# Masking query tile 1 of an attention max pass on VectorE: one fused instruction a head in place of a shared plain maximum

## The chip, the cores and the metric

The kernel runs on one core of a Trainium2 chip. The metric is the device time of one execution in microseconds, as the median of several executions. The core's engines are TensorE (PE in the profile; PEld is its weight load), VectorE (DVE), ScalarE (ACT), GpSimd (POOL) and SyncE (SP), which issues the DMAs. Each runs its own list of instructions in order, and they wait for one another at semaphores.

## The reference

Eight sequences of 512 tokens with 256 features go through one transformer block with its norms behind the sums:

```
qkv = x @ Wqkv + bqkv                      # 16 heads of 16
scores = q @ k.T / 4 + alibi_causal_bias   # -(i-j)*slope for j <= i, -inf for j > i
attn = softmax(scores) @ v
x1 = layernorm(x + attn @ Wo + bo)
up, gate = x1 @ ternary(W_up).T, x1 @ ternary(W_gate).T
out = layernorm(x1 + (silu(up) * gate) @ ternary(W_down).T)
```

The causal mask is what matters here: query i must not see key j > i, neither in the sum nor in the maximum that the softmax subtracts.

## The kernel before

Each batch (one sequence) goes through two passes of scores. The **max pass** computes each query's largest score, the exp pass computes the scores again, transposed, with that maximum already subtracted by rows of the stacked operands, and takes the exponential.

The heads go in four quads of four. In the max pass of a quad the scores of a head and of one tile of 128 queries are one product: queries on the 128 partitions, the keys 0 to 128 * (tile + 1) - 1 along the columns, so 128, 256, 384 or 512 columns. Function `max_unit` groups these into 11 units a quad, each filling a PSUM bank as far as it goes: unit 0 is query tile 0 of all four heads (4 x 128 columns), units 1 and 2 are query tile 1 of two heads each (2 x 256), units 3 to 6 are tile 2 of one head (384), units 7 to 10 tile 3 of one head (512). Step `max.G.N` is the products of unit N in quad G on TensorE (L477), step `take.G.N` the maximum on VectorE. Two banks, `max_bank0` and `max_bank1`, take the units in turn: TensorE waits for `max_drained` of the unit two before, VectorE for `max_filled` of its own.

Only the last 128 columns of a unit's head cross the diagonal. They are masked in one of two ways, by the constant `MASK_BY_DVE`:

- For query tiles below it TensorE adds the mask: behind each head's product it multiplies an identity by a 128x128 tile `causal` (0 or -1e30) into the last 128 columns (L480). VectorE then takes one plain maximum over the whole unit, a `tensor_reduce` with as many results as heads (L731).
- For query tiles from it on, VectorE adds `causal_wide` (bf16, the mask in its last 128 columns and 0 before) and takes the negated maximum in one fused instruction, `tensor_tensor_reduce` (L727). The sums are written back into the bank, and the maximum is fetched by a second, short instruction, the accumulator read, which the profile lists at the same line and which gives the bank back.

When all 11 units of a quad are taken, `mt.G` transposes the maxima on TensorE (L489), `mt_out.G` splits them in two bf16 parts on VectorE (L741, L743), and SyncE copies them into `q_stack` for the exp pass of that quad.

The order of work on all engines is one list written out by hand: `FIRST_ORDER` for the first batch, `LOOP_ORDER` for batches 1 to 7, each of which also ends the batch before (its last exponentials, the products with v, output projection, norms, feed-forward part), `LAST_ORDER` for that tail alone. Each engine walks the list and does its own part of each step. Around quads 0 to 2 the list interleaves the max pass with the feed-forward steps of the batch before: `up.M` and `gate.M` on TensorE (L555), `swish.M` (L784) and `swiglu.M` (L794) on VectorE, `down.M` on TensorE (L568) into the two accumulator banks; `qk_rest` and `x1_hi` parts on ScalarE, `x1_lo` (L776) and `v_out` (L714) on VectorE. Around quads 2 and 3 it interleaves the exp pass of quads 0 and 1 (L495 on TensorE, L610 on ScalarE, masks by GpSimd at L855) and `pv`, the products with v (L508). All banks but the two max banks and the two accumulators are a ring of four, used in list order; each is given back by the instruction that empties it. In the loop, for instance, `gate.4` takes the bank that `gate.3` had and `swiglu.3` emptied.

A few lines of the loop's order around the change, quad 1 to quad 3:

```
down.0 max.1.2 swish.2 take.1.0 gate.3 swiglu.2 ... mt.0 take.1.1 take.1.2 ... swish.3 ... max.1.3 up.4
max.1.4 take.1.3 up.5 max.1.5 stack_read.1 swiglu.3 gate.4 max.1.6
up.7 take.1.10 exp.0.2 take.2.0 exp.0.3 swiglu.5 take.2.1 max.2.3 take.2.2 load_next max.2.4 gate.6
mt_out.2 take.3.1 max.3.2 exp.1.2 take.3.2 exp.1.3 max.3.3 exp.1.4 down.7
```

Of the kernel before, what the change touches and what calls it, by code (L numbers as in the profile page):

```python
# [11 lines left out]
ALU = mybir.AluOpType  # L12
# [4 lines left out]
BATCH, SEQ, HID = 8, 512, 256  # L17
# [11 lines left out]
LOWEST_START = 3e38  # L29
# [11 lines left out]
GROUP = 40  # L41

RING = 4
MASK_BY_DVE = 2
EXP_UNITS = 10
MAX_UNITS = 11

# [1 line left out]
def max_unit(n):  # L49

    if n == 0:
        return [0, 1, 2, 3], 0
    if n < 3:
        return [2 * (n - 1), 2 * (n - 1) + 1], 1
    return ([n - 3], 2) if n < 7 else ([n - 7], 3)
# [95 lines left out]
def block_kernel(nc, x, w_qkv, b_qkv, b_qkv_cols, w_o, b_o, w_up_t, w_gate_t, w_down_t, k_const, q_const, out, scratch):  # L151
    ctx = ExitStack()
    with ctx:
        def sb(name, shape, dt):
            return ctx.enter_context(nc.sbuf_tensor(name, shape, dt))

        def sem(name):
            return ctx.enter_context(nc.semaphore(name))
# [13 lines left out]
        causal_wide = sb("causal_wide", [P, SEQ], BF16)  # L172
# [15 lines left out]
        neg_max = sb("neg_max", [P, QUADS, P], F32)  # L188
# [28 lines left out]
        max_bank = [ctx.enter_context(nc.psum_tensor(f"max_bank{i}", [P, 512], F32)) for i in range(2)]  # L217
# [6 lines left out]
        max_drained = [sem(f"max_drained{i}") for i in range(2)]  # L224
# [99 lines left out]
        def max_at(g, n):  # L324

            u = g * MAX_UNITS + n
            return u % 2, u // 2
# [101 lines left out]
        def _(pe):  # L429
            def body(steps, it):  # L430
# [3 lines left out]
                for step in steps:  # L434
# [30 lines left out]
                    elif kind == "max":  # L465
# [9 lines left out]
                        for i, h in enumerate(heads):  # L475
                            o = max_bank[k][:, width * i:width * (i + 1)]
                            mm = pe.matmul(o, q_stack[0:MAX_ROW, 4 * g + h, P * tile:P * (tile + 1)],  # L477
                                           k_stack[0:MAX_ROW, 4 * g + h, 0:width], start=True, stop=tile >= MASK_BY_DVE)
                            if tile < MASK_BY_DVE:
                                mm = pe.matmul(o[:, width - P:width], ident_bf[:, :], causal[:, :], start=False, stop=True)  # L480
# [165 lines left out]
        def _(dve):  # L646
# [29 lines left out]
            def body(steps, it):  # L676
# [3 lines left out]
                for step in steps:  # L680
# [23 lines left out]
                    elif kind == "pv" and step[1] >= 2 and step[2] == TT - 1:  # L704
                        g = step[1]
# [11 lines left out]
                    elif kind == "take":  # L717
                        _, g, n = step
                        k, use = max_at(g, n)
                        heads, tile = max_unit(n)  # L720
                        width = P * (tile + 1)
                        at_least(dve, max_filled[k], MAX_PER_BANK, it, use + 1)
                        first_col = 4 * heads[0] + tile
                        if tile >= MASK_BY_DVE:
                            dve.sem_inc(dve_passed, 1)
                            scores = max_bank[k][:, 0:width]
                            dve.tensor_tensor_reduce(  # L727
                                scores, scores, causal_wide[:, SEQ - width:SEQ], -1.0, LOWEST_START, ALU.add, ALU.min,
                                neg_max[:, g, first_col:first_col + 1]).then_inc(max_drained[k], 1)
                            continue  # L730
                        dve.tensor_reduce(  # L731
                            neg_max[:, g, first_col:first_col + 4 * (len(heads) - 1) + 1:4],
# [2 lines left out]
                    elif kind == "mt_out":  # L735
                        g = step[1]
# [8 lines left out]
                    elif kind == "nt_out":  # L745
                        g = step[1]
# [3 lines left out]
                        heads = rg.bank(nt)[:, :].rearrange("p (s c) -> p s c", c=32)  # L750
# [74 lines left out]
                    elif kind == "ternary" and step[1] < 2:  # L825
                        i = step[1]
# [5 lines left out]
                                                 op0=ALU.is_gt, op1=ALU.subtract).then_inc(ternary_done, 1)  # L832

            iterations(dve, body)


# [137 lines left out]
```

## Time and profile before

| | |
|---|---|
| runs of the kernel | 634.56 us median of 3 (634.03 to 636.05) |
| the profiled execution | 636.64 us, span in the profile 634.7 us |
| mean granted TensorE clock | 0.967 of full |
| PE busy | 582.3 us, 92% of the span |
| DVE busy | 502.0 us, 79% |
| ACT busy | 307.1 us, 48% |
| POOL busy | 296.5 us, 47% |

Busy times are averages over stages with different limits. A record of an instruction reaches from its start to the acknowledged end of its writing, and the next one often starts before that; start-to-start times tell how long an engine is really held. Times of the timeline are in microseconds from the span's start.

### The profile page before, as it was taken

Reading aid. Unit: us, or ns where it says so; the run is one execution under the profiler, and the core shown is the slowest. Engines: PE = TensorE matmul, PEld = TensorE weight load, DVE = VectorE, ACT = ScalarE, POOL = GpSimd, SP = SyncE. Lnnn points to the kernel's source line nnn. Section 1 sums busy time; section 2 is a strip of 40 time slices with the busy share of each in tenths; the row PEclk is TensorE's granted clock in tenths of the full one; section 3 lists DMA queues with packets and bytes.
Section 4 is the critical chain, followed back from the end, with each engine's and each line's share of the span. In section 5 each row is a group of like instructions: output and inputs, shape, how many; then the busy total and the mean of one; then the engine's idle time right before and its main releaser. Section 6 shows DMA issues by size and latency. Waiting matters only on the chain.

```text
span 634.7 us, 13198 instructions
## 1 busy us (share of the span) xinstructions
PE 582.3 (92%) x4027; PEld 339.6 (54%) x4066; DVE 502.0 (79%) x1271; ACT 307.1 (48%) x543; POOL 296.5 (47%) x494
## 2 busy tenths in 40 slices
PE   6477899999999999999999999999999999998694
PEld 3243346664656556664656556664656656663343
DVE  4367968997699968997699968997699968995454
ACT  1144542477245742387245743477245743477151
POOL 1307683274544563264544563264544563275233
PEclk9767999999999999999999999999999999999987
DMA  8952155502761065502761065502761065502000
GB/s 212 311 191 65 35 166 169 134 3 75 215 174 34 1 193 171 133 1 69 221 174 34 1 198 166 133 1 74 216 174 34 1 207 158 133 1 68 1 1 33
DMA packets 48096, 69.42 MB, mean 109 GB/s; under 512 B 4784, under 2 KB 44208, under 8 KB 44976
## 3 DMA queue, kind: packets, MB, share of 16 engines
q1 hardware_dynamic: 48080, 69.22, 37.3%
q8 instruction: 8, 0.13, 0.1%
q14 instruction: 8, 0.07, 0.0%
HBM read 39.59 MB, written 29.36 MB: 109 GB/s over the span
## 4 chain that ended last, share of the span: by engine, by line
PE 59%; DMA 15%; DVE 13%; issue 6%; ACT 3%; POOL 2%; SPq 1%; POOLq 0%; DVEq 0%
PE ring L555 18%; PE max_bank L477 10%; DMA k_stack<-k_slots 9%; PE acc L568 8%; PE ring L495 6%; PE ring L457 5%; PE acc L508 5%; DMA k_slots<-qk_parts 3%; PE max_bank L480 2%; DMA q_stack<-max_parts 2%; DVE y L660 2%; PE ring L462 1%; DVE qk_rest L690 1%; DVE qk_rest L699 1%; POOL rstd L881 1%
## 5 line engine op out<-in xcount | busy, mean ns | idle before, releaser
L610 ACT ACTIVATE probs<-ring 128x512 f32<-128x512 f32 x320 | 171.4, 601 | 88.2 <-PE ring L495 55.4
L855 POOL TENSOR_SCALAR_AFFINE_SELECT probs<-probs 128x256 f32<-128x256 f32 (+1 forms) x320 | 121.1, 403 | 165.2 <-ACT probs L610 164.1
L727 DVE CUSTOM_DVE_ANT_0 max_bank<-max_bank,causal_wide 128x384 f32<-128x384 f32 (+1 forms) x256 | 158.3, 636 | 9.5 <-PE max_bank L477 6.8
L477 PE MATMUL max_bank<-k_stack,q_stack 112*128 112x384 bf16 (+3 forms) x512 | 137.3, 312 | 20.8 <-DMA k_stack<-k_slots 11.8
L885 POOL TENSOR_TENSOR hidden_lo<-hidden,hidden_hi 128x512 f16<-128x512 f32 x64 | 74.1, 1159 | 77.1 <-ACT hidden_hi L640 76.9
L495 PE MATMUL ring<-q_stack,k_stack 128*128 128x128 bf16 (+3 forms) x473 | 93.9, 297 | 6.8 <-DMA q_stack<-max_parts 5.3
L477 PEld LDWEIGHTS max_bank<-k_stack,q_stack 112*128 112x128 bf16 x512 | 50.6, 99 | 61.9 <-DVE neg_max L727 21.5
L629 ACT ACTIVATE gating<-ring,tanh_scale 128x512 f32<-128x512 f32 x64 | 44.0, 687 | 74.6 <-PE ring L555 74.6
L508 PE MATMUL acc<-probs,v_ones 128*32 128x512 f32 (+3 forms) x1024 | 78.2, 437 | 0.1
L495 PEld LDWEIGHTS ring<-q_stack,k_stack 128*128 128x128 bf16 x512 | 46.5, 100 | 57.2 <-issue 21.2
L731 DVE TENSOR_REDUCE neg_max<-max_bank 128x2 f32<-128x512 f32 (+1 forms) x96 | 63.3, 686 | 13.4 <-PE max_bank L480 13.1
L457 PE MATMUL ring<-x_t,wqkv 128*128 128x512 f32 x128 | 63.1, 619 | 1.6 <-DVE x_t L684 1.2
L568 PE MATMUL acc<-tern_down,hidden_hi 128*128 128x256 f16 x256 | 59.0, 272 | 0.4
L568 PE MATMUL acc<-tern_down,hidden_lo 128*128 128x256 f16 x256 | 59.0, 272 | 0.0
L508 PEld LDWEIGHTS acc<-probs,v_ones 128*32 128x32 f32 x1024 | 28.4, 109 | 42.0 <-issue 36.4
L784 DVE SCALAR_TENSOR_TENSOR gating<-gating,ring 128x512 f32<-128x512 f32 x64 | 43.1, 683 | 4.7 <-ACT gating L629 4.5
L794 DVE SCALAR_TENSOR_TENSOR hidden<-gating,ring 128x512 f32<-128x512 f32 x64 | 43.7, 682 | 3.6 <-POOL hidden_lo L885 2.6
L640 ACT ACTIVATE hidden_hi<-hidden 128x512 f16<-128x512 f32 x64 | 40.2, 628 | 9.8 <-DVE hidden L794 9.7
L480 PE MATMUL max_bank<-causal,ident_bf 128*128 128x128 bf16 x256 | 44.4, 227 | 0.0
L601 ACT ACTIVATE qk_parts<-ring,bias_cols 128x512 bf16<-128x512 f32 x16 | 11.0, 688 | 66.7 <-PE ring L457 66.7
L881 POOL TENSOR_TENSOR rstd<-var_eps,half_neg 128x4 f32<-128x4 f32 x16 | 16.3, 1019 | 53.0 <-DVE var_eps L674 53.0
L555 PE MATMUL ring<-x_hi,tern_up 128*128 128x512 f16 x128 | 39.0, 386 | 0.7 <-issue 0.7
(93 smaller groups left out, 877.6 us busy)
## 6 DMA issues: line engine op xcount, KB each, us to landing
q_stack<-qk_scratch SPq DMA_DIRECT2D x16, 768.0 KB, 5.9
k_stack<-k_slots SPq DMA_DIRECT2D x16, 768.0 KB, 8.2
qk_scratch<-qk_parts SPq DMA_DIRECT2D x16, 384.0 KB, 5.2
k_slots<-qk_parts SPq DMA_DIRECT2D x16, 384.0 KB, 3.2
xin<-x_dram SPq DMA_DIRECT2D x9, 512.0 KB, 3.5
qk_scratch<-qk_parts SPq DMA_DIRECT2D x16, 256.0 KB, 2.8
k_slots<-qk_parts SPq DMA_DIRECT2D x16, 256.0 KB, 3.0
res<-x_dram SPq DMA_DIRECT2D x8, 512.0 KB, 4.0
```

The costliest lines, as they stand in the source:

```text
L457: mm = pe.matmul(bank[:, :], wqkv[:, f, col:col + P], x_t[:, f, :], start=(f == 0), stop=(f == FT - 1))
L477: mm = pe.matmul(o, q_stack[0:MAX_ROW, 4 * g + h, P * tile:P * (tile + 1)], k_stack[0:MAX_ROW, 4 * g + h, 0:width], start=True, stop=tile ...
L480: mm = pe.matmul(o[:, width - P:width], ident_bf[:, :], causal[:, :], start=False, stop=True)
L495: mm = pe.matmul(bank[:, col:col + SEQ - P * j], k_stack[:, 4 * g + h, P * j:P * (j + 1)], q_stack[:, 4 * g + h, P * j:SEQ], start=True, s ...
L508: mm = pe.matmul(acc[g % 2][32 * h:32 * (h + 1), P * j:SEQ], v_ones[:, j, 4 * g + h, :], probs[:, g % 2, n, col:col + SEQ - P * j], start= ...
L555: mm = pe.matmul(bank[:, :], w[:, f, P * m:P * (m + 1)], part[:, f, :], start=(f == 0 and part is x1_hi), stop=(f == FT - 1 and part is x1 ...
L568: mm = pe.matmul(acc[t // 2][:, HID * (t % 2):HID * (t % 2 + 1)], part[:, m, P * t:P * (t + 1)], tern_down[:, m, :], start=(m == 0 and par ...
L610: rg.drained(act.activation(probs[:, g % 2, n, :], rg.bank(step)[:, :], ACT.Exp), step)
L727: dve.tensor_tensor_reduce(scores, scores, causal_wide[:, SEQ - width:SEQ], -1.0, LOWEST_START, ALU.add, ALU.min, neg_max[:, g, first_col: ...
L731: dve.tensor_reduce(neg_max[:, g, first_col:first_col + 4 * (len(heads) - 1) + 1:4], max_bank[k][:, 0:width * len(heads)].rearrange("p (h ...
L855: return pool.affine_select(out=v, in_=v, compare_op=ALU.is_ge, fill=0.0, base=0, pattern=([[0, blocks]] if blocks > 1 else []) + [[1, P]] ...
L885: pool.tensor_tensor(hidden_lo[:, m, :], hidden[:, m % 2, :], hidden_hi[:, m, :], ALU.subtract).then_inc(hidden_split, 1)
```

## The change

The constant goes from 2 to 1, and VectorE's branch goes over the heads of a unit, since a fused instruction gives one maximum only. For units 1 and 2 of each quad TensorE issues the two products without the two mask products, and VectorE issues two fused instructions of 128x256, one for each head, in place of one plain maximum over 128x512. The bank is given back by the second one. Unit 0 keeps TensorE's mask and the plain maximum; tiles 2 and 3 are as before. The order of steps is not changed.

```diff
-MASK_BY_DVE = 2
+MASK_BY_DVE = 1
...
                         if tile >= MASK_BY_DVE:
                             dve.sem_inc(dve_passed, 1)
-                            scores = max_bank[k][:, 0:width]
-                            dve.tensor_tensor_reduce(
-                                scores, scores, causal_wide[:, SEQ - width:SEQ], -1.0, LOWEST_START, ALU.add, ALU.min,
-                                neg_max[:, g, first_col:first_col + 1]).then_inc(max_drained[k], 1)
+                            for i in range(len(heads)):
+                                scores = max_bank[k][:, width * i:width * (i + 1)]
+                                ins = dve.tensor_tensor_reduce(
+                                    scores, scores, causal_wide[:, SEQ - width:SEQ], -1.0, LOWEST_START, ALU.add, ALU.min,
+                                    neg_max[:, g, first_col + 4 * i:first_col + 4 * i + 1])
+                            ins.then_inc(max_drained[k], 1)
                             continue
```

## Rows read from the trace of the kernel before

**Rows 1.** The page: busy tenths in 40 slices, then the chain by engine.

```profile
PE   6477899999999999999999999999999999998694
DVE  4367968997699968997699968997699968995454
...
PE 59%; DMA 15%; DVE 13%; issue 6%; ACT 3%; POOL 2%; SPq 1%; POOLq 0%; DVEq 0%
```

**Rows 2.** Busy time in windows: first batch's front, one loop batch, its middle.

```profile
core 0: us, PE busy (x) PEld busy (x) DVE busy (x) ACT busy (x) POOL busy (x), PEclk, DMA share, GB/s
27.00:95.00 68.00, 55.68 (x345) 27.27 (x350) 50.40 (x120) 30.52 (x52) 37.10 (x49) 0.83 0.42 134
315.00:387.00 72.00, 70.54 (x510) 42.02 (x514) 61.58 (x160) 37.41 (x67) 34.72 (x60) 1.00 0.38 111
322.00:342.00 20.00, 19.95 (x132) 11.86 (x133) 19.86 (x52) 8.55 (x14) 5.66 (x6) 1.00 0.51 142
```

**Rows 3.** Timeline of PE, quad 2: start, length, line, operation, tiles, shapes.

```profile
341.58 0.22 PE L480 MATMUL max_bank<-causal,ident_bf 128*128 128x128 bf16 x1
341.64 0.59 PE L555 MATMUL ring<-x_hi,tern_up 128*128 128x512 f16 x2
...
342.93 0.49 PE L477 MATMUL max_bank<-k_stack,q_stack 112*128 112x384 bf16 x2
...
344.14 0.34 PE L477 MATMUL max_bank<-k_stack,q_stack 112*128 112x384 bf16 x1
```

**Rows 4.** Timeline of PE, quad 0 of the first batch.

```profile
28.04 0.31 PE L480 MATMUL max_bank<-causal,ident_bf 128*128 128x128 bf16 x1
28.15 0.42 PE L477 MATMUL max_bank<-k_stack,q_stack 112*128 112x256 bf16 x1
```

**Rows 5.** Groups of instructions, shapes apart: busy us, mean ns, idle before.

```profile
L727 DVE CUSTOM_DVE_ANT_0 max_bank<-max_bank,causal_wide 128x512 f32<-128x512 f32 x128 | 87.8, 705 | 1.9 <-PE max_bank L477 0.3
...
L727 DVE CUSTOM_DVE_ANT_0 max_bank<-max_bank,causal_wide 128x384 f32<-128x384 f32 x128 | 71.1, 567 | 7.5 <-PE max_bank L477 6.5
...
L731 DVE TENSOR_REDUCE neg_max<-max_bank 128x2 f32<-128x512 f32 x64 | 42.1, 684 | 0.8 <-PE max_bank L480 0.8
```

**Rows 6.** Timeline of DVE, quad 2.

```profile
340.47 0.69 DVE L731 TENSOR_REDUCE neg_max<-max_bank 128x4 f32<-128x512 f32 x1
...
341.66 1.29 DVE L731 TENSOR_REDUCE neg_max<-max_bank 128x2 f32<-128x512 f32 x2
343.45 0.57 DVE L727 CUSTOM_DVE_ANT_0 max_bank<-max_bank,causal_wide 128x384 f32<-128x384 f32 x1 [0.51 <-PE max_bank L477]
343.94 0.14 DVE L727 DVE_READ_ACCUMULATOR2_ANT neg_max<- 128x1 f32 x1
343.94 0.60 DVE L727 CUSTOM_DVE_ANT_0 max_bank<-max_bank,causal_wide 128x384 f32<-128x384 f32 x1
...
344.45 0.68 DVE L784 SCALAR_TENSOR_TENSOR gating<-gating,ring 128x512 f32<-128x512 f32 x1
```

**Rows 7.** Timeline of DVE, quad 1.

```profile
330.52 1.28 DVE L731 TENSOR_REDUCE neg_max<-max_bank 128x2 f32<-128x512 f32 x2
331.72 0.68 DVE L784 SCALAR_TENSOR_TENSOR gating<-gating,ring 128x512 f32<-128x512 f32 x1
...
332.79 0.68 DVE L794 SCALAR_TENSOR_TENSOR hidden<-gating,ring 128x512 f32<-128x512 f32 x1
...
333.86 0.14 DVE L727 DVE_READ_ACCUMULATOR2_ANT neg_max<- 128x1 f32 x1
334.06 0.57 DVE L727 CUSTOM_DVE_ANT_0 max_bank<-max_bank,causal_wide 128x384 f32<-128x384 f32 x1
```

**Rows 8.** Timeline of PE, quad 1.

```profile
333.70 0.60 PE L555 MATMUL ring<-x_hi,tern_gate 128*128 128x512 f16 x2
```

**Rows 9.** Timeline of DVE, quad 3.

```profile
351.65 1.28 DVE L731 TENSOR_REDUCE neg_max<-max_bank 128x2 f32<-128x512 f32 x2
```

**Rows 10.** Timeline of PE, quad 3.

```profile
352.48 0.33 PE L477 MATMUL max_bank<-k_stack,q_stack 112*128 112x384 bf16 x1
```

## The prediction

> **What bounds the kernel now.** I read the page first, for the mix of engines over time. Outside the start and the end TensorE's slices read 9. VectorE reads 9 too, in three or four slices of each batch: those in which the max pass and the feed-forward part overlap. The chain that ended last is TensorE's for 59% and VectorE's for 13% [rows 1]. Then the windows: the first batch ran at a mean granted clock of 0.83, with TensorE waiting often; a loop batch (315 to 387) ran at 1.00 and shows 70.5 us of busy TensorE and 61.6 us of busy VectorE in 72.0; in its overlapping part, 322 to 342, they show 19.95 and 19.86 us of the 20 [rows 2]. Such figures are inflated, because a record overlaps the next one: a 128-column mask product has a record of 0.22 us, and yet the next matmul starts 0.06 us after it [rows 3]. So I went by start-to-start times, in the timeline of that one batch (batch 4 of 0 to 7; the other loop batches repeat it within hundredths). There too each engine starts one instruction straight behind another, with pauses of 0.2 us at most. Two engines are full at once, and they hand two score banks back and forth in a fixed order. So what decides is not which engine has less work, but at which hand-off one waits for the other.
>
> **What goes.** Per batch 16 products of the causal tile for query tile 1 (2 units x 2 heads x 4 quads), each 0.06 us of TensorE at full clock (341.58 to 341.64 [rows 3]); I take 0.058, the mean over a row of them. That is 0.23 us per quad, 0.93 per batch, 6.5 over seven batches. In the first batch a mask takes 0.11 us (28.04 to 28.15 [rows 4]), the lower clock level, so 1.7 us there: 8.2 us in all for 128 mask products.
>
> **What comes.** 64 plain maxima of 128x512 (684 ns each [rows 5]) give way to 128 fused instructions of 128x256, which the trace does not have. The nearest rows are 384 wide (567 ns) and 512 wide (705 ns) [rows 5]: 138 ns for 128 elements, so a record of 429 ns at 256 wide. The next instruction starts 0.08 us before a fused record ends (343.45 + 0.57 = 344.02 against the next start at 343.94 [rows 6]), so the slot is 0.345 us. A fused instruction directly behind a fused one takes some 0.02 to 0.04 us longer (0.49, then 0.51 us from 343.94 to 344.45 [rows 6]); I take 0.035. A unit of two heads then occupies VectorE for 0.345 + 0.035 + 0.345 = 0.725 us, where the plain maximum takes 0.60 (two of them have a common record of 1.29 us, one alone of 0.69 [rows 6]). The two units of a quad follow each other, mostly with nothing between: 0.725 + 0.035 + 0.725 = 1.485 us in place of 1.20, so +0.285 per quad, +1.1 per batch. The lower bound of the new slot is its 256 elements alone, 0.276 us (a gain of 0.05 per unit against 0.60); the upper bound is the slot of the 384-wide one, 0.49 (+0.38 per unit). I take 0.345, since two rows give a line through it.
>
> The bank is given back later too. A plain maximum gives it back with its record, 0.69 us after its start. A fused one gives it back with its accumulator read, which starts where the slot ends and takes 0.14 us [rows 6]; TensorE's next product into that bank starts 0.06 us later (343.45 + 0.49 + 0.14 = 344.08, product at 344.14 [rows 3]). For the pair that is 0.345 + 0.38 + 0.14 = 0.865 us after its start, 0.18 later than now. No DMA, no bank and no wait is added; what changes is how late existing waits clear.
>
> The Trainium skill (Perfetto Trace Analysis, Optimizing Scalar/DVE Operations) puts a VectorE instruction's overhead on PSUM at about 125 ns and advises grouping. Here the rows leave 0.07 us (0.345 less 0.276). With the page's figure each half would take 0.40 us and the forecast below would be about 1.6 us later; this trace does not agree with it, and the sum goes by the rows.
>
> **Through one batch, quad by quad** (shifts against now).
>
> Quad 0: VectorE's extra 0.25 us falls beside ScalarE's x1_hi, for which VectorE waits before x1_lo, and TensorE's x_lo part of up.0 waits for that in turn. Two masks fewer stand ahead of qk.3, which feeds that ScalarE work. I take half of their 0.12 us: -0.06. Without that cover the 0.25 us would arrive in full.
>
> Quad 1: take.1.1 starts at 330.52 and VectorE is never idle from there to 334. Swish.3 (331.72) and swiglu.3 (332.79) come 0.285 us later [rows 7]. Swiglu.3 now ends at 333.47 (332.79 + 0.68) and frees the ring bank that gate.4 takes at 333.70 [rows 8]; it would end at 333.76, plus 0.06 for the hand-off: 333.81. So TensorE comes out of quad 1 about 0.10 us late, its 0.23 us of saved slots used up in waiting. VectorE's pause of 0.2 us (from 333.86, where an accumulator read starts that any next instruction could run beside, to 334.06 [rows 7]) takes in the rest of its delay, and both engines are at +0.10.
>
> Quad 2: take.2.1 starts at 341.66, and take.2.2 gives its bank back at 341.66 + 1.29 = 342.95 [rows 6]. Max.2.4, the second of the pair of products at 342.93, starts at 343.10, straight behind max.2.3 (a common record of 0.49, where one of 384 columns has 0.34 alone) [rows 3]. After the change take.2.2 starts 0.76 us after take.2.1 and gives back 0.865 us later: 343.29, the product at 343.35, +0.25; with the 0.10 from quad 1 it is +0.35. TensorE could have been there 0.23 us early; that is lost, and gate.6 and down.4 stand in the queue right behind it.
>
> Quad 3: take.3.1 starts at 351.65 [rows 9], with the shift at 352.00. Its bank is wanted by max.3.3 at 352.48, which starts as TensorE's queue comes to it [rows 10]. After the change: 352.00 + 0.865 + 0.06 = 352.93, so +0.44. Behind it stand exp.1.4 and down.7; down.7 ends the accumulators, which first the second norm and then pv.0 need, and TensorE has no room before pv.0 at 355.4.
>
> From pv.0 the chain goes over ScalarE, GpSimd's masks and rstd, VectorE's normalised output, mt_out.3 and its DMA to the next batch's first products. I found no pause in TensorE's timeline there that could take the delay in, so I carry it over whole. Per batch: 0.44 - 0.06 = +0.38; over seven, +2.7 us.
>
> First batch: at the lower clock a mask is worth 0.11 us, and the maxima of a quad's two-head units wait for their own products. Removing four masks per quad (0.43 us) pays for the 0.285 us more of VectorE. But the third quad waits for a stack transfer and the last one runs at full clock. I take 0; ends -1.7 (all masks) and +1.1. The last pass has no max work: 0.
>
> Sum: the profiled execution took 636.6 us around a span of 634.7; with +2.7 it would be 639.3 around 637.4. Its own time is 2.1 us above the median of the runs, 634.56, so the forecast for the median is 634.56 + 2.7, which I round to **637.2**.
>
> **Rivals.** About 0.3% (1.9 us) is what this kernel's measurement can tell from no change; below, "same" is within that.
>
> 1. *Hand-offs, as above*: chance 0.43. Own range 635.9 to 639.5: lower if half of each shift is taken in, upper if the quads' shifts add undiminished.
>
> 2. *VectorE paces the whole max pass*: every 0.285 us arrives, 32 quads x 0.285 = 9.1, giving 643.7. For it: VectorE's full windows [rows 2]. Against: its pause of 0.51 us before 343.45, a wait for TensorE [rows 6], and others of 0.2 us behind it. It decides if these close. Chance 0.13.
>
> 3. *Both effects cancel*: TensorE's saved 0.93 us per batch fills the waits that VectorE's later releases make, 634.6 (within 1.5). It holds if VectorE arrives in quad 2 some 0.3 us ahead of where it does now, or if the pair releases its bank after 0.7 us. Chance 0.25.
>
> 4. *TensorE paces, faster*: the slots saved in quads 0 and 1 reach the end, 8 x 0.058 x 7 = 3.2 us, plus 0.9 in the first batch: 630.5; with all four quads, 8.2 us, 626.4. For it: TensorE's 9s in almost every slice and its 59% of the chain [rows 1]. Against: max.2.4 and max.3.3 start within 0.16 us of their banks' release today (342.95 to 343.10, 352.34 to 352.48) [rows 3, 6, 9, 10]. It decides where VectorE has room at those places. Chance 0.19. The Trainium skill (TensorE: Matmul & The Clock Gate, Back-to-back issue gap) gives about 81 ns per 128-column matmul in a stream with weight loads. That would make this rival's full gain 9 us in the loop instead of 6.5; the rows here say 0.06 us, so the trace does not agree.
>
> That the masks would stay on TensorE can't be: both sides of the edit go by the same constant.
>
> **How the numbers follow.** Predicted is rival 1's 637.2. Slower by over 0.3%: nearly all of 1 and all of 2, 0.54. Same: 3 and a little of 1, 0.27. Faster: 0.19. The range of 631.0 to 641.5 leaves out most of 2 and the larger gains of 4, under 0.2 together.
>
> **What would show it.** 128 fused records of 128x256 near 430 ns, some 0.38 us apart within a pair; mask products down to 128. In each loop batch max.2.4 and max.3.3 start 0.06 us behind an accumulator read, with a TensorE gap of 0.3 us or more before them, and gate.4 behind swiglu.3. VectorE's pauses near 343 and 353 shrink. The period from batch to batch, 71.4 us (max.0.0 starts at 172.75 in batch 2 and at 458.28 in batch 6), would become about 71.8. The prediction is wrong if the 256-wide slot is far from 0.345 us, if TensorE shows no new gap at those three places, or if a gap elsewhere, in the part behind pv.0, takes the delay in.

## The result, and the profile after

The changed kernel takes 659.37 us in the median (656.6 to 665.02), the kernel before 634.48: 1.0387 times, with a 95% interval of 1.0348 to 1.0426. That is 25 us more between the medians, nine times what was forecast, and far outside the range. The profiled execution took 659.4 us around a span of 657.3, where before it was 636.64 around 634.7.

The page of the changed kernel, lines that answer to [rows 1], and the lines on the queues that carry instructions:

```profile
PE   6367899998999899998999989998999989999694
...
DVE  4386859996699758996699958995699957996454
...
q14 instruction: 38, 0.31, 0.2%
q8 instruction: 8, 0.13, 0.1%
...
PE 59%; DVE 20%; issue 12%; DMA 6%; DVEq 1%; POOL 1%; ACT 1%; SPq 1%; POOLq 0%
```

and the same queues on the page of before:

```profile
q8 instruction: 8, 0.13, 0.1%
q14 instruction: 8, 0.07, 0.0%
```

Both pages look alike where I had looked. What differs is a line that I had not read: q14 brought 38 packets of instructions (8 KB each: 0.31 MB over 38) in place of 8, and the chain spends 12% of the span in "issue", where it was 6% [rows 1]. Of these two only the queue's line holds up as a sign: the experiments below have kernels with 9 packets and 11% "issue", and others with 38 or 39 packets and 7 or 8%. The DMA view of the window from 160 to 590 us, which lies inside the loop, from its second turn on, says when the packets come. For the kernel before it has no line for q14 at all; for the changed kernel it has this one, and three of the packets start within 226 to 233, around a jump back that is looked at below:

```profile
q14 instruction: 26, 0.21, 0.2%
```

The groups by shape, with the new form (compare [rows 5]):

```profile
L728 DVE CUSTOM_DVE_ANT_0 max_bank<-max_bank,causal_wide 128x256 f32<-128x256 f32 x128 | 50.9, 453 | 0.2
```

A 256-wide record takes 453 ns, where the line through two rows said 429; two in three directly follow a fused one and are the longer kind. Quad 2 of the batch that [rows 6] showed, VectorE:

```profile
353.43 0.42 DVE L728 CUSTOM_DVE_ANT_0 max_bank<-max_bank,causal_wide 128x256 f32<-128x256 f32 x1
353.77 0.14 DVE L728 DVE_READ_ACCUMULATOR2_ANT neg_max<- 128x1 f32 x1
353.77 0.47 DVE L728 CUSTOM_DVE_ANT_0 max_bank<-max_bank,causal_wide 128x256 f32<-128x256 f32 x1
...
354.91 0.14 DVE L728 DVE_READ_ACCUMULATOR2_ANT neg_max<- 128x1 f32 x1
355.03 0.57 DVE L728 CUSTOM_DVE_ANT_0 max_bank<-max_bank,causal_wide 128x384 f32<-128x384 f32 x1
```

and TensorE there (compare [rows 3]):

```profile
354.50 0.33 PE L477 MATMUL max_bank<-k_stack,q_stack 112*128 112x384 bf16 x1
355.11 0.34 PE L477 MATMUL max_bank<-k_stack,q_stack 112*128 112x384 bf16 x1 [0.28 <-DVE neg_max L728]
355.29 0.60 PE L555 MATMUL ring<-x_hi,tern_gate 128*128 128x512 f16 x2
```

The first of the pair takes 0.34 us to the next start, the second, behind a fused one, 0.38. The last accumulator read of take.2.2, the unit behind it, ends at 354.91 + 0.14 = 355.05, and max.2.4 starts 0.06 us later, at 355.11, with an idle time of 0.28 us in front: the hand-off that was forecast, though the gap is a little under the 0.3 us that was named for it.

The 22.6 us of the span are elsewhere. I took the starts of max.0.0, the first product of each batch's max pass, from the timelines. From batch 1 to batch 7 they are 449.4 us apart (102.50 to 551.93), where before they were 428.2 (101.08 to 529.23): 74.9 us a batch in place of 71.4. Of these 3.5 us, quads 1 and 2 hold 0.13 and 0.14 and quad 0 on average 0.3; the other 3 us lie between the start of quad 3 and the next batch. There VectorE's timeline has this, at the end of the loop's second turn:

```profile
226.08 0.42 DVE L755 TENSOR_TENSOR attn<-ring,inv_sum 128x256 f32<-128x256 f32 x1
229.48 0.69 DVE L684 COPY x_t<-ring 128x512 f32<-128x512 f32 x1 [2.97 <-issue]
```

while before the same two instructions stand so:

```profile
222.05 0.42 DVE L753 TENSOR_TENSOR attn<-ring,inv_sum 128x256 f32<-128x256 f32 x1
222.89 0.69 DVE L684 COPY x_t<-ring 128x512 f32<-128x512 f32 x1 [0.41 <-PE ring L446]
```

The copy of x_t is VectorE's first data instruction of a turn. Its input had been ready since 226.89, when TensorE's transposes for it ended (225.81 + 1.08 in TensorE's timeline); nothing that the profile shows was waited for. The chain that ended last goes straight through it (L334 is the loop):

```profile
226.17 0.07 DVEq L334
226.24 3.13 issue
229.37 0.06 DVEq L334
229.43 0.04 issue
229.48 0.70 DVE x_t L684
```

VectorE's sequencer, the part of the engine that goes through its list, reaches the jump back at 226.17 and has its next entry 3.1 us after it. The list of waits (total us, number, longest) has that six times, once for each jump taken, and TensorE's waits for x_t behind it:

```profile
DVE x_t L684 <- issue: 16.7, 6, 3.0
PEld ring L457 <- DVE x_t L684: 13.6, 6, 2.5
PE ring L457 <- DVE x_t L684: 12.5, 7, 2.1
```

It costs more than its own length in some turns. Windows of 4 us behind that jump, the columns as in [rows 2]:

```profile
226.00:230.00 4.00, 1.71 (x12) 0.91 (x10) 0.99 (x3) 2.66 (x5) 1.61 (x5) 0.95 0.41 135
230.00:234.00 4.00, 3.69 (x6) 1.45 (x7) 0.17 (x1) 0.00 (x0) 0.00 (x0) 0.50 0.01 4
234.00:238.00 4.00, 4.00 (x13) 1.70 (x11) 3.69 (x6) 1.37 (x3) 1.67 (x3) 0.69 0.36 123
```

After its pause TensorE was granted 0.50 of full clock, the lower of its two levels (1.2 GHz), from 230 to 234 and in part of the next window. qk.0 and qk.1's four products of 512 columns took 3.75 us there, where they took 1.88 us before (224.05) and 1.95 us in the turn at 381, in which the clock stayed at 1.00. The lower clock came behind three of the six jumps (at 226, 451 and 526). From one max.0.0 to the next, the batches with these three took 4.1 to 5.6 us more than the 71.36 of before, the others 2.1 to 2.7.

### The profile page after: what moved, and what is told of

It reads as the page before. It is cut to its first block, busy times and chain, and to the rows that moved or that the text cites. A ratio compares the mean times of both kernels' runs of the same rounds, so it can differ in the third digit from the quotient of the medians.

```text
span 657.3 us, 13237 instructions
## 1 busy us (share of the span) xinstructions
PE 588.7 (90%) x3938; PEld 330.7 (50%) x3938; DVE 511.3 (78%) x1463; ACT 307.6 (47%) x543; POOL 295.5 (45%) x494
## 4 chain that ended last, share of the span: by engine, by line
PE 59%; DVE 20%; issue 12%; DMA 6%; DVEq 1%; POOL 1%; ACT 1%; SPq 1%; POOLq 0%
PE ring L555 12%; PE acc L508 10%; PE max_bank L477 8%; PE ring L495 7%; PE ring L457 7%; DVE max_bank L728 6%; PE acc L568 5%; DMA k_stack<-k_slots 3%; PE ring L462 3%; DVE neg_max L728 3%; PE ring L517 2%; PE ring L533 2%; DVE z L766 1%; DVE x L660 1%; DMA k_slots<-qk_parts 1%
## 5 line engine op out<-in xcount | busy, mean ns | idle before, releaser
L728 DVE CUSTOM_DVE_ANT_0 max_bank<-max_bank,causal_wide 128x384 f32<-128x384 f32 (+2 forms) x384 | 209.5, 576 | 6.2 <-PE max_bank L477 3.2
L477 PE MATMUL max_bank<-k_stack,q_stack 112*128 112x384 bf16 (+3 forms) x512 | 135.4, 315 | 23.8 <-DMA k_stack<-k_slots 13.0
L495 PE MATMUL ring<-q_stack,k_stack 128*128 128x512 bf16 (+3 forms) x512 | 106.7, 305 | 7.5 <-DMA q_stack<-max_parts 6.6
L477 PEld LDWEIGHTS max_bank<-k_stack,q_stack 112*128 112x128 bf16 x512 | 48.5, 100 | 77.2 <-DVE neg_max L728 35.0
L457 PE MATMUL ring<-x_t,wqkv 128*128 128x512 f32 x128 | 68.1, 660 | 12.5 <-DVE x_t L684 12.5
L629 ACT ACTIVATE gating<-ring,tanh_scale 128x512 f32<-128x512 f32 x64 | 44.0, 687 | 75.4 <-PE ring L555 75.3
L728 DVE DVE_READ_ACCUMULATOR2_ANT neg_max<- 128x1 f32 x384 | 54.9, 143 | 0.0
L457 PEld LDWEIGHTS ring<-x_t,wqkv 128*128 128x128 f32 x128 | 24.4, 209 | 34.9 <-issue 20.7
```

Of the source, the lines that this page charges most:

```text
L457: mm = pe.matmul(bank[:, :], wqkv[:, f, col:col + P], x_t[:, f, :], start=(f == 0), stop=(f == FT - 1))
L495: mm = pe.matmul(bank[:, col:col + SEQ - P * j], k_stack[:, 4 * g + h, P * j:P * (j + 1)], q_stack[:, 4 * g + h, P * j:SEQ], start=True, s ...
L629: act.activation(gating[:, m % 2, :], rg.bank(step)[:, :], ACT.Tanh, scale=tanh_scale[:, 0:1]).then_inc(tanh_done, 1)
L728: ins = dve.tensor_tensor_reduce(scores, scores, causal_wide[:, SEQ - width:SEQ], -1.0, LOWEST_START, ALU.add, ALU.min, neg_max[:, g, firs ...
```

## The experiments

The explanation before the first run: VectorE's loop got longer by 32 recorded instructions (from 275 to 307 between two jumps, counting all entries that the trace recorded, semaphore and register entries too; a unit of query tile 1 has five entries, a semaphore increment, two fused instructions and two accumulator reads, where it had one), and so did its list ahead of the loop. Perhaps the loop no longer stays in the memory that the engine runs its instructions from. The rival: the loss is what the fused maxima do to the banks. Ratios are against the kernel before on the same chip. A filler is an entry put in for its length alone; all are `dve.sem_inc(dve_passed, 1)`, put where VectorE waits.

**same_size.** No mask moved; VectorE's list made as long as in the changed kernel.

```diff
 # kernel before; take step, first batch, g == 0 and n == 0
+                            for _ in range(32):
+                                dve.sem_inc(dve_passed, 1)
 # pv step of quad 2, ahead of its wait; in the loop and in the last pass
+                            for _ in range(32):
+                                dve.sem_inc(dve_passed, 1)
```

> The kernel before, with 32 more semaphore increments in VectorE's list ahead of the loop (at the first maximum, where VectorE is idle for 10 us) and 32 more inside the loop (ahead of the wait for the accumulator of quad 2, where it is idle for 1 to 2 us), so that its list is as long as that of the changed kernel before and inside the loop; no mask is moved. Theory A (VectorE's longer loop no longer stays in its instruction buffer, so each turn fetches instructions again and stalls some 3 us at the jump back): about 22 us slower than before, 653 to 660, with some 30 more instruction packets on q14 than the 8 KB ones of before. Theory B (the two fused maxima and the bank hand-offs make the whole loss): no change, 634 to 635.5, since increments run while the engine waits.

Measured: 1.0297 (1.0248 to 1.0346), 39 packets on q14:

```profile
DVE x_t L684 <- issue: 16.9, 6, 3.1
```

Theory A's case came. Part of the loss may be the increments themselves, about 3 us a turn (in the timeline of after_ahead50 they start 0.093 us apart), in a place with less idle time than that; the next run has no such doubt.

**ahead32.** Only the 32 ahead of the loop (the first hunk above).

> The kernel before, with 32 semaphore increments more in VectorE's list ahead of the loop alone. Theory A1 (blocks touched): no change at 634 to 635.5 if 275 recorded instructions still fit from the new place, else 650 to 660; the place is not known, I take 60 to 40 for no change. Theory A2 (size alone) and theory B: no change, 634 to 635.5.

Measured: 1.0324 (1.0280 to 1.0368), 38 packets, the same six waits. The loop is, instruction for instruction, the loop of before; only its place in VectorE's list moved by 32:

```profile
DVE x_t L684 <- issue: 16.8, 6, 3.0
```

I had given 60 to 40 for no change; the other case came. Since this loop has no fused maxima for tile 1 and is no longer than before, its size alone and the hand-offs are ruled out as the cause of the large part.

**after_ahead50.** The changed kernel with 50 increments ahead of the loop.

> The changed kernel, with 50 semaphore increments more in VectorE's list ahead of the loop (at the first maximum of the first batch, where VectorE is idle) and nothing changed in the loop. Theory A1 (what counts is how many 128-instruction blocks of 8 KB the loop touches; 50 instructions shift the loop to a place where 307 recorded instructions touch one block fewer): the stalls at the jump back go away and what stays is the cost in the max pass, 636.5 to 638. Theory A2 (the number of instructions in the loop alone is over the buffer's size, wherever it starts): stays at 655 to 662. Theory B (hand-offs): stays at 655 to 662, with no stall that goes away.

Measured: 1.0074 (1.0052 to 1.0096), 640.59 against 636.61 us. It has eighteen more fillers than ahead32 and a longer loop, and the stall is gone. The fillers cost VectorE nothing themselves: they run from 17.1 to 22.1 us, and its first maximum starts at 28.57. VectorE at the same jump, and the page's queue line:

```profile
224.15 0.42 DVE L758 TENSOR_TENSOR attn<-ring,inv_sum 128x256 f32<-128x256 f32 x1
224.99 0.69 DVE L684 COPY x_t<-ring 128x512 f32<-128x512 f32 x1 [0.41 <-PE ring L446]
```

```profile
q14 instruction: 9, 0.07, 0.0%
```

The hand-off is unchanged beside it: 

```profile
345.81 0.34 PE L477 MATMUL max_bank<-k_stack,q_stack 112*128 112x384 bf16 x1 [0.28 <-DVE neg_max L731]
```

So of the 3.9% of the change 0.7% is what it does to the work (0.5 to 1.0 by the interval), and the other 3.1% is where it puts the loop.

**ahead128, ahead64, ahead16, after_ahead96.** Four runs on the rule that this suggests: the list comes in blocks of 128 instructions (8 KB packets, if an instruction takes 64 bytes), and the loop stays in place when it touches at most three of them. Each is the edit of ahead32 with another number (the 128 are spread over three places of the first batch where VectorE waits: 90, 19 and 19); after_ahead96 has the changed kernel under it.

> The kernel before, with 128 semaphore increments more in VectorE's list ahead of the loop (90, 19 and 19 at three places of the first batch where VectorE is idle). Theory A1 (place of the loop among blocks of 128 instructions): 128 is one whole block, so the loop starts at the same place in its block as before, and the time is that of before within 0.5%, without fetches in the loop, although 32 such increments cost 3%. Theory A3 (any instruction more ahead of the loop harms it, by a full buffer): as slow as with 32, or slower, 3% or more.

> The kernel before with 64 increments ahead of the loop. Theory A1 in numbers: let o be the place of the loop's first instruction in its block of 128 and L its recorded length; the loop stays in the buffer when it touches three blocks, o + L at most 384. Before (L 275) fits, with 32 more ahead it doesn't, with 50 more ahead the changed one (L 307, 32 more ahead by the change itself) fits: that leaves o between 78 and 95. With 64 ahead the place is 14 to 31: fits, 634 to 638, no instruction packets between 160 and 590 us. Theory A4 (every filler that is not a whole block costs): 650 to 660.

> The kernel before with 16 increments ahead of the loop. A1: the place is 94 to 111 and the limit for 275 is 109, so it most likely fits (634 to 638, and then o is at most 93); if it doesn't, 650 to 660, and o is 94 or 95. A4: 650 to 660.

> The changed kernel with 96 increments ahead of the loop. A1: its own 32 and the 96 make 128, so the place is o again, 78 to 95, and the limit for 307 is 77: it doesn't fit, 655 to 662, with five instruction packets a turn, although 50 increments made it fit. A5 (any filler of 50 or more ahead relieves the changed kernel): 638 to 642.

| run | loop, recorded | moved by | ratio (95%) | packets on q14 |
|---|---|---|---|---|
| before | 275 | 0 | 1 | 8 |
| ahead16 | 275 | 16 | 1.0006 (0.9980 to 1.0032) | 8 |
| ahead32 | 275 | 32 | 1.0324 (1.0280 to 1.0368) | 38 |
| ahead64 | 275 | 64 | 0.9989 (0.9966 to 1.0012) | 8 |
| ahead128 | 275 | 128 | 1.0006 (0.9980 to 1.0031) | 9 |
| changed kernel | 307 | 32 | 1.0387 (1.0348 to 1.0426) | 38 |
| after_ahead50 | 307 | 82 | 1.0074 (1.0052 to 1.0096) | 9 |
| after_ahead96 | 307 | 128 | 1.0429 (1.0345 to 1.0514) | 39 |

Every run fell as the rule said. 16, 64 and 128 more are free and 32 are not; 50 cure the changed kernel and 96 don't. With the place of the loop's first instruction in its block between 78 and 93, all eight lines follow from "place plus length at most 384". Before, ahead32, the changed kernel and after_ahead50 suggested the rule and ahead16 could only narrow the place, so ahead64, ahead128 and after_ahead96 are its tests. The last has two executions only, but its interval starts at 1.0345, where that of after_ahead50 ends at 1.0096. The rule counts recorded instructions; if the loop has entries that the trace does not record, the place is that much lower.

The Trainium skill names the mechanism (Runtime: NRT & Kernel Launch, Instruction fetch mechanics): an engine's instructions are streamed into a small memory in blocks, and a taken branch whose target isn't in the current window forces a fetch of the target before execution can go on. The trace agrees with that: 16.7 us in six stalls. The same section of the Trainium skill gives blocks of 16 KiB, 256 instructions, and this case's trace does not agree there: on q14 the packets have 8 KB, and after_ahead96 decides it. With blocks of 256, of which the loop may touch two, the first seven lines of the table would follow too, but then 128 would carry a loop of 307 away from the block's end, and it would have fitted.

**both_masks.** VectorE's half of the change alone, at the fitting place: TensorE keeps its mask for tile 1, added a second time without effect.

```diff
 # after_ahead50
-                                           k_stack[0:MAX_ROW, 4 * g + h, 0:width], start=True, stop=tile >= MASK_BY_DVE)
-                            if tile < MASK_BY_DVE:
+                                           k_stack[0:MAX_ROW, 4 * g + h, 0:width], start=True, stop=tile >= 2)
+                            if tile < 2:
```

> The changed kernel with the 50 increments ahead of the loop, but TensorE still adds its mask to query tile 1 too (added twice, the result is the same). So VectorE's half of the change alone, at the fitting place. The run without these masks was 1.0074 times before. Theory H (the hand-offs bind in quads 1 to 3, so what TensorE saves is mostly lost in waiting): at most 2.5 us slower than that, 1.007 to 1.012. Theory P (TensorE's slots pace the kernel, and only they kept the loss small): the full 8 us more, 1.019 to 1.022.

Measured: 1.0079 (1.0055 to 1.0104). Without the masks it was 1.0074. The difference can't be told from none, and by the two intervals it is 2.4 us at most, where all mask products together were priced at 8.2: most of what TensorE saves is lost once the fused maxima are there. Quads 1 and 2 take 10.82 and 10.44 us in both, to the hundredth; of the three, quad 0 alone shows a difference (12.85 us in most turns, 12.72 or 12.75 without the masks).

**no_mask.** TensorE's half alone: kernel before, mask products of tile 1 left out, VectorE's list untouched. It leaves out part of the causal mask.

```diff
 # kernel before
-                                           k_stack[0:MAX_ROW, 4 * g + h, 0:width], start=True, stop=tile >= MASK_BY_DVE)
-                            if tile < MASK_BY_DVE:
+                                           k_stack[0:MAX_ROW, 4 * g + h, 0:width], start=True, stop=tile >= 1)
+                            if tile < 1:
```

> The kernel before, with the mask products of query tile 1 left out and VectorE's plain maximum over both heads kept: it leaves out the causal mask of tile 1 in the max pass. So TensorE's half of the change alone; VectorE's list is not touched. Theory P (TensorE paces): all slots arrive, 8.2 us faster, 0.987. Theory H (VectorE and the banks bind in quads 1 to 3): 1 to 4 us faster, 0.9935 to 0.9985.

Measured: 0.9933 (0.9907 to 0.9958), 4.3 us. A quad takes 0.17 to 0.20 us less, of the 0.23 that TensorE saves. Theory P's 0.987 lies outside the interval; the value itself lies just beyond the end of theory H's range. So with the plain maxima about half of the sum of all slots arrives, the most that theory H allowed.

**quad0.** The change in quad 0 of the loop alone, where cover was seen; an attempt at a version better than both.

```diff
+# used in place of the comparison with MASK_BY_DVE, on TensorE and on VectorE
+def mask_by_dve(it, g, tile):
+    return tile >= (1 if g == 0 and not isinstance(it, int) else MASK_BY_DVE)
```

> The change in quad 0 of the loop batches alone, 8 instructions more in the loop and none ahead of it. With 50 increments ahead the changed kernel's quad 0 took 0.13 us less per loop batch than before and its quads 1 and 2 0.12 and 0.14 more. Theory A1: 283 recorded instructions still fit (the run with 32 ahead bounds the room to between 289 and 306), so 0.1 us per batch is won: 0.998 to 1.001. If it doesn't fit: 1.03 or so.

Measured: 0.9983 (0.9960 to 1.0005), 8 packets on q14. The loop fits. Quad 0 took 12.72 us in three turns of seven and 12.81 to 13.33 in the others (12.85 in six before), and the time can't be told from that of before. No version faster beyond doubt was found.

## Why the prediction was wrong

**The step that failed** is the sentence "No DMA, no bank and no wait is added; what changes is how late existing waits clear." The change lengthens VectorE's list, 32 entries in the loop and 32 ahead of it, and that adds instruction transfers and a wait at each jump back. No row that I gave speaks of it; the page's queue lines and the length of the loop would have. I counted each instruction's duration and not that it is an entry in a list. In its place the runs showed a stall of 2.8 us on average at each of six jumps back and 30 more packets of instructions, 3.1% of the time; ahead32 has them without any change to the masks, and after_ahead50 loses them with the change in place. Nor did a rival hold it: rival 2, the only one well above the forecast, gave 643.7 by another mechanism, 1.4% over 634.56, and after_ahead50 and both_masks lie at 1.0% at most by their intervals.

**The 256-wide slot** was right: 0.34 to 0.35 and 0.38 us, against 0.345 and 0.38.

**The hand-offs** came as priced, by starts in batch 4 of the changed kernel. Quad 1 (from max.1.0 to max.2.0) takes 0.13 us more, forecast 0.10. There the waits are spread more than I said. TensorE loses 0.17 us at max.1.3, which starts 0.06 us behind the accumulator read of take.1.1, and 0.10 at up.5, which waits for swish.3's bank. Gate.4, the only one that I had named, does start 0.05 us behind swiglu.3 (345.46), but loses only 0.03 more. In quad 2 max.2.4 comes 4.16 us behind max.2.0 (350.95 to 355.11), before 3.91 (339.19 to 343.10): the +0.25 of the forecast, of which 0.11 is won back before quad 3, which I had not foreseen. In quad 3 max.3.3 comes 3.15 us behind max.3.0 (361.39 to 364.54) in place of 2.99, +0.16 for a forecast of +0.09. Its gap is 0.23 us, where 0.3 or more was forecast. Together 0.43 at that point, forecast 0.44. Quad 0, forecast at -0.06, has no single value: in after_ahead50 it is -0.13 to -0.10 in five of seven turns and +0.5 in one, in the changed kernel it is -0.13 and -0.07 in two turns and +0.2 to +0.5 in the five others. What makes the long ones was not looked for.

**The sum for the loop**, 0.38 us a batch, is right where the loop stays in place: in after_ahead50 max.0.0 of batch 1 starts at 102.81 and of batch 7 at 533.34, 71.76 us a batch against 71.36, so +0.40. (One batch of it has 0.6 us more in quad 0 than the others; the terms of the sum are less sure than their total.) That the two agree to 0.02 is luck: the prediction took the loop batches to repeat within hundredths, which holds for quads 1 and 2, but from quad 3 to the next batch they differ by up to 0.7 us in the kernel before, and in ahead16, ahead64 and ahead128, with the same loop, the period is 71.33, 71.13 and 71.26. The forecast of +2.7 us stands against 4.0 us between the medians in that run, and 3.3 to 6.1 by the interval of the ratio. The **first batch**, taken at 0, is a mis-sized term too: its max.0.0 to that of batch 1 takes 75.3 us in after_ahead50, 74.1 before. It takes 72.9 to 74.1 in seven profiles that still have the plain maxima there (all but same_size, whose fillers in the loop fall in that stretch), with VectorE's list moved by 0 to 128 entries, and 74.9 to 76.1 in the four with the fused maxima. So some 0.8 us or more come with the fused maxima, and not with the place of the list; what makes them was not looked for.

**Two readings** were off without consequence: VectorE's line has two or three 9s a batch and not three or four, and of the 16 masks of the first batch 12 take 0.107 us and the four of the last quad 0.06, 1.5 us together and not 1.7.

**That TensorE's saving is lost** was right for most of it, and is shown by both_masks. My reason, that TensorE waits for banks that VectorE gives back later, is what the timelines show, with the waits of quad 1 as said above. The weight of VectorE's pauses was right as well: its later work used them up.

**What stays open**: how many blocks the memory holds and how far ahead it fetches (three blocks fit and four touched do not, five packets a turn then come), and that q14's packets are VectorE's, which is inferred from runs in which its list alone was changed. Why the lower clock came in some turns and not in others is open as well; the length of the pause doesn't sort them (1.99 us without it at the first jump, 1.76 us with it at the fifth).

## What to carry to other kernels

Before adding instructions to an engine's loop, count that engine's list, the part ahead of the loop and the loop itself, and read the page's instruction queues: if packets stop after the loop's first turns and come again only behind it, as here before the change, the loop stays where the engine runs it, and a few entries more in front can end that. After such a change look first at the jump back ("issue" in front of a turn's first instruction in the list of waits, and not the chain's share of "issue"), and try some fillers ahead of the loop before judging the change itself. Between two engines that are both full, an edit that takes from one and gives to the other is priced at the hand-offs; here most of 0.23 us a quad saved on one was lost beside 0.29 us added on the other.

## What the runs showed that was not expected

- 32 semaphore increments in idle time ahead of a loop made the whole kernel 3.2% slower, and 16, 64 or 128 of them did nothing.
- A jump back in a loop that no longer stays in place held VectorE for 2.8 us on average (16.7 over 6) and 2.97 at most by the list of waits; in the kernel before it doesn't show, since the wait behind the jump, 0.41 us, is for TensorE.
- After 2.07 us without products TensorE was granted 0.50 of full clock for more than 4 us in one turn of the changed kernel, and 1.00 throughout in another after 1.99 us; where the lower clock came, the batch lost 4.1 to 5.6 us in place of 2.1 to 2.7.
